# Decoder layer on one core: unread products in the opening waits, four contexts moved, an expert matrix folded into the second projection, and both gate halves in one operand

## What is computed

```
# 1. self-attention, B,T = 2,256 folded on (8,128) tokens; 32 heads of 16, 8 key/value heads, RoPE, causal
x = x + attn(layernorm(x), Wq, Wk, Wv, Wo)
# 2. cross-attention on ctx (8,128,512) joined with the layer-normalised x: 256 keys, 32 heads of 128, 4 key/value heads
x = x + xattn(layernorm(x), ctx, Wq, Wk, Wv, Wo)
# 3. feed-forward, on h = layernorm(x)
logits = h @ gate_w                                # 512 x 8
r      = sum(top_k(logits, 2))                     # one number a token
shared = relu(h @ up_w) ** 2 @ down_w              # 512 -> 1024 -> 512
routed = ((h @ fc1_w) @ expert_w) * r @ fc2_w      # 512 -> 256 -> 256 -> 512
x = x + layernorm(shared + routed) * gamma + beta
```

## Time and profile before

| | us |
|---|---|
| median of 3 runs (lowest, highest) | 1036.62 (1036.33, 1036.84) |
| the profiled execution, its own time | 1037.11 |
| its span, first to last instruction | 1035.4 |
| PE busy | 1015.5 (98% of the span) |
| DVE busy | 644.1 (62%) |
| ACT busy | 525.8 (51%) |
| POOL busy | 384.8 (37%) |
| mean granted TensorE clock | 0.998 |

### The profile page before, as it was taken

How to read it: one execution, slowest core, us unless ns; L and a number is a source line. 1 busy time by engine, 2 the same in 40 slices (tenths; PEclk the granted TensorE clock), 3 DMA queues, 4 the chain that set the end, 5 groups by cost and what they waited for, 6 DMA issues and landing times.

```text
span 1035.4 us, 15896 instructions
## 1 busy us (share of the span) xinstructions
PE 1015.5 (98%) x5656; PEld 854.4 (83%) x5656; DVE 644.1 (62%) x1305; ACT 525.8 (51%) x1593; POOL 384.8 (37%) x370
## 2 busy tenths in 40 slices
PE   6999999999999999999999999999999999999997
PEld 6777777777888888888888888888888888799996
DVE  6888888878435655556555456555546578466554
ACT  5666667666525645445455446454436556422211
POOL 3545444444132433224433225433226356311110
PEclk9999999999999999999999999999999999999999
DMA  9300111104552221202212102121202213100000
GB/s 336 113 21 22 41 41 42 41 21 143 164 154 68 65 71 42 91 22 68 65 41 72 62 26 87 42 82 32 71 32 82 91 62 103 42 1 20 20 21 21
DMA packets 70105, 68.38 MB, mean 66 GB/s; under 512 B 3984, under 2 KB 53904, under 8 KB 70032
## 3 DMA queue, kind: packets, MB, share of 16 engines
q1 hardware_dynamic: 70032, 67.43, 20.8%
HBM read 48.55 MB, written 18.87 MB: 65 GB/s over the span
## 4 chain that ended last, share of the span: by engine, by line
PE 94%; DVE 3%; DMA 1%; issue 1%; ACT 0%; SPq 0%; DVEq 0%; POOLq 0%; POOL 0%
PE bank L224 27%; PE bank L226 26%; PE bank L225 26%; PE bank L981 5%; PE bank L753 3%; PE bank L715 1%; PE bank L719 1%; DVE b_nb L1591 1%; DMA rawQ<-in_L_attn_Wq_dram 1%; PE bank L722 1%; PE bank L725 1%; PE bank L633 0%; DVE b_max L1588 0%; DVE PTl L1345 0%; PE bank L668 0%
## 5 line engine op out<-in xcount | busy, mean ns | idle before, releaser
L570 POOL TENSOR_TENSOR Pb<-Pb,b_rec 128x512 f32<-128x512 f32 x128 | 133.6, 1044 | 349.8 <-DVE b_rec L1595 348.6
L1588 DVE TENSOR_REDUCE b_max<-bank 128x2 f32<-128x512 f32 x128 | 87.8, 686 | 84.4 <-PE bank L226 84.2
L1087 ACT ACTIVATE PTh<-bank 128x512 fp32r<-128x512 f32 x128 | 76.2, 595 | 115.5 <-PE bank L981 114.8
L1229 ACT ACTIVATE Pb<-bank,b_nb 128x256 f32<-128x256 f32 x256 | 119.2, 475 | 15.7 <-DVE b_nb L1591 15.5
L1144 ACT ACTIVATE Pa<-bank,a_nb 128x128 f32<-128x128 f32 x256 | 90.4, 367 | 42.9 <-DVE a_nb L1468 42.1
L224 PE MATMUL bank<-WOh,Oh 128*128 128x512 f32 x256 | 110.7, 432 | 1.0 <-DVE x_res L1605 0.9
L532 POOL TENSOR_TENSOR Pa<-Pa,a_rec 128x512 f32<-128x512 f32 x64 | 68.2, 1066 | 104.6 <-DVE a_rec L1474 104.0
L224 PE MATMUL bank<-XTh,WQh 128*128 128x512 f32 x256 | 101.6, 397 | 0.0
L226 PE MATMUL bank<-WOh,Ol 128*128 128x512 f32 x256 | 100.9, 394 | 0.0
L225 PE MATMUL bank<-WOl,Oh 128*128 128x512 f32 x256 | 100.4, 392 | 0.0
L226 PE MATMUL bank<-XTh,WQl 128*128 128x512 f32 x256 | 100.0, 390 | 0.0
(11 more groups left out here) (230 smaller groups left out, 2706.3 us busy)
## 6 DMA issues: line engine op xcount, KB each, us to landing
kv_scratch<-KVst SPq DMA_DIRECT2D x64, 256.0 KB, 2.9
KV<-kv_scratch SPq DMA_DIRECT2D x32, 512.0 KB, 3.4
raw<-in_L_xattn_Wo_dram SPq DMA_DIRECT2D x32, 256.0 KB, 3.3
raw<-in_L_xattn_Wq_dram SPq DMA_DIRECT2D x24, 256.0 KB, 4.0
cx<-in_ctx_dram SPq DMA_DIRECT2D x8, 256.0 KB, 9.1
raw_first<-in_L_xattn_Wq_dram SPq DMA_DIRECT2D x8, 256.0 KB, 4.7
raw<-in_L_ffn_up_w_dram SPq DMA_DIRECT2D x8, 256.0 KB, 4.0
raw<-in_L_ffn_down_w_dram SPq DMA_DIRECT2D x8, 256.0 KB, 2.6
```

What stands on the lines that cost most here:

```text
L570: gp.tensor_tensor(pk, pk, b_rec[:, k % 4, :].unsqueeze(2).to_broadcast([P, 2, KEYS]), ALU.mult).then_inc(b_g_norm, 1)
L1087: return act.activation(dst, src, ACT.Copy)
L1229: op = act.activation(Pb[:, k % 4, h, :], bank[k % 3][:, h * KEYS:(h + 1) * KEYS], ACT.Exp, bias=b_nb[:, k % 4, h:h + 1], scale=X_SCALE, a ...
L1588: dve.tensor_reduce(b_max[:, k % 4, :], bank[k % 3][:].rearrange("p (h k) -> p h k", h=2), AX.X, ALU.max).then_inc(b_v_mx, 1)
```

## The change

Six edits are made together.

1. DVE makes `ident_r`, the identity in float32r, first of all, and fills its two zeroed value buffers after it. PE then begins with `warm_up(9, 7)`: nine products of 512 columns of the identity with itself into bank 7, which nobody reads, ahead of its wait for the first weights; and `warm_up(7, 1)`, seven such products into bank 1, behind `turn_xn(0)`, ahead of the wait for the query weights.
2. In the opening PE makes the second half of `unit(0)` ahead of `turn_k(0)` and not behind it, and the contexts 4, 5 and 6 ahead of `unit(3)`; ACT and DVE take these contexts' parts accordingly, ahead of the parts of unit 3.
3. The expert matrix is not split as it comes. It is loaded apart (`ex_raw`), transposed in four pieces at the end of step 26 of the last group (`turn_expert`), split, and multiplied with `fc2` once (`expert_product`, 12 products of 512 columns, ahead of `out_piece(g, 7, 0)`). The result, split again, takes the place of `fc2`. The expert product of every pair, its high part on ACT and its low part on DVE go away, and the last product takes `LTh`, `LTl` directly.
4. The gate's high and low part lie in one operand `GT`, in columns 0 to 7 and 8 to 15, so that two multiplications a chunk do for three; DVE adds the two halves of the logits with a reduction where it had copied them.
5. `LN3_STEPS` are 8 and 12 where they were 14 and 16.
6. The down weights of the last group take the steps 26 to 30 where they had 27 to 31, the expert weight step 26.

```diff
@@ PE, the opening
+            def warm_up(count, bk):
+                for _ in range(count):
+                    pe.matmul(bank[bk][:].rearrange("p (c k) -> p c k", c=SG), ident_r[:],
+                              ident_r[:].unsqueeze(1).to_broadcast([P, SG, P]), start=True, stop=True)
+
+            pe.wait_ge(v_c, 1)
+            warm_up(9, 7)
             pe.wait_ge(g_const, 6)
             pe.wait_ge(ld_kv, 32)
             for n in range(2):
                 turn_weights(n)
             turn_xn(0)
+            warm_up(7, 1)
             pe.wait_ge(ld_q, 16)
...
             turn_q(0)
+            unit(0, (2, 3))
             turn_k(0)
-            unit(0, (2, 3))
             unit(1)
...
             scores(0, 1)
-            unit(3)
             pe.wait_ge(v_w, 10)
             turn_context(4)
             turn_context(5)
             turn_context(6)
+            unit(3)
+
             pe.wait_ge(v_ul, 3)
             turn_context(7)
@@ PE, the last group and the feed-forward
+            def turn_expert():
+                pe.wait_ge(b_v_q, XG + 2 * XG * XKV - XG)
+                pe.wait_ge(ld_ex, 16)
+                for mc in range(LC):
+                    for lc in range(LC):
+                        op = pe.transpose(bank[6][:, mc * LAT + lc * P:mc * LAT + (lc + 1) * P],
+                                          ex_raw[:, lc, mc * P:(mc + 1) * P], ident[:])
+                op.then_inc(c_pe_e, 1)
+
+            def expert_product():
+                pe.wait_ge(c_v_e, 1)
+                pe.wait_ge(b_a_exp, DUOS * XKV)
+                pe.wait_ge(b_g_w, ffn_ready(NUP + NFC - 1))
+                for lc, bk in enumerate((6, 1)):
+                    for mc in range(LC):
+                        op = split3(pe, bank[bk][:], EXTh[:, mc, lc * P:(lc + 1) * P], EXTl[:, mc, lc * P:(lc + 1) * P],
+                                    F2h[:, mc, :], F2l[:, mc, :], mc == 0, mc == LC - 1)
+                op.then_inc(c_pe_e, 1)
...
+                    if last and k == EX_STEP:
+                        turn_expert()
+                if last:
+                    expert_product()
                 out_piece(g, NB - 1, 0)
                 outputs(g, QUADS - 1)
...
                 for kc in range(KC):
-                    op = split3(pe, bank[0][:, 0:KEYS], GTh[:, kc, :], GTl[:, kc, :], X3h[:, kc, :], X3l[:, kc, :],
-                                kc == 0, kc == KC - 1)
+                    pe.matmul(bank[0][:, 0:KEYS], GT[:, kc, :], X3h[:, kc, :], start=kc == 0, stop=False)
+                    op = pe.matmul(bank[0][:, 0:KEYS], GT[:, kc, :], X3l[:, kc, :], start=False, stop=kc == KC - 1)
...
-                    if n == 1:
-                        pe.wait_ge(b_g_w, ffn_ready(NUP + NFC))
-                        pe.wait_ge(c_v_l, 2 * c + 1)
-                        for m in range(LC):
-                            for kc in range(LC):
-                                op = split3(pe, bank[1][:, m * KEYS:(m + 1) * KEYS], EXh[:, kc, m * P:(m + 1) * P],
-                                            EXl[:, kc, m * P:(m + 1) * P], LTh[:, kc, :], LTl[:, kc, :],
-                                            kc == 0, kc == LC - 1)
-                        op.then_inc(c_pe_e, 1)
-                pe.wait_ge(c_v_l, 2 * c + 2)
+                pe.wait_ge(c_v_l, c + 1)
@@ DVE
+            dve.wait_ge(g_const, 5)
+            dve.tensor_copy(ident_r[:], ident[:]).then_inc(v_c, 1)
+            dve.wait_ge(g_const, 6)
+            dve.tensor_copy(mask_r[:], mask_f[:]).then_inc(v_c, 1)
             dve.memset(f32(Vbdh[:]), 0.0).then_inc(v_c, 1)
             dve.memset(f32(Vbdl[:]), 0.0).then_inc(v_c, 1)
-            dve.wait_ge(g_const, 6)
-            dve.tensor_copy(ident_r[:], ident[:]).then_inc(v_c, 1)
-            dve.tensor_copy(mask_r[:], mask_f[:]).then_inc(v_c, 1)
...
+                        if k == EX_STEP:
+                            dve.wait_ge(c_a_e, 1)
+                            lo(EXTl[:].rearrange("p m n -> p (m n)"), bank[6][:],
+                               EXTh[:].rearrange("p m n -> p (m n)")).then_inc(c_v_e, 1)
+                if last:
+                    for lc, bk in enumerate((6, 1)):
+                        dve.wait_ge(c_a_e, 2 + lc)
+                        lo(F2l[:, lc, :], bank[bk][:], F2h[:, lc, :]).then_inc(c_v_e, 1)
                 outputs(g, QUADS - 1)
...
-                        dve.tensor_copy(logits[:], bank[0][:, KEYS:2 * KEYS].rearrange(
-                            "p (t n) -> p t n", t=2)[:, :, 0:NE])
+                        halves = bank[0][:, KEYS:2 * KEYS].rearrange("p (t s n) -> p t n s", t=2, n=NE)[:, :, :, 0:2]
+                        dve.tensor_reduce(logits[:], halves, AX.X, ALU.add)
@@ SP, behind the self-attention
             sp.dma_start(gate_raw[:], gate_w.rearrange("(k p) n -> p k n", p=P)).then_inc(ld_gate, 16)
+            sp.dma_start(ex_raw[:], expert_w.rearrange("(k p) n -> p k n", p=P)).then_inc(ld_ex, 16)
```

More of the change, by code:

```diff
@@ L193, in decoder_layer @@
         HBl = sb("HBl", "Q", 24, [IC, KEYS], F32R)
-        EXh = sb("EXh", "KV", 8, [LC, LAT], F32R)
-        EXl = sb("EXl", "KV", 10, [LC, LAT], F32R)
+        EXTh = sb("EXTh", "KV", 8, [LC, LAT], F32R)
+        EXTl = sb("EXTl", "KV", 10, [LC, LAT], F32R)
         xn3 = sb("xn3", "F", 0, [2, D])
-        GTh = sb("GTh", "F", 4, [KC, P], F32R)
-        GTl = sb("GTl", "F", 6, [KC, P], F32R)
+        GT = sb("GT", "F", 4, [KC, P], F32R)
+        ex_raw = sb("ex_raw", "F", 6, [LC, LAT])
         gate_raw = sb("gate_raw", "F", 8.5, [KC, NE])
@@ L297, in chunk_steps @@
                 steps += [(22 + i - NUP, "ffn", i) for i in range(NUP, NUP + NFC)]
-                steps += [(26, "ffn", NUP + NFC)]
-                steps += [((17, 19, 21, 27, 28, 29, 30, 31)[c], "ffn", NUP + NFC + 1 + c) for c in range(IC)]
+                steps += [((17, 19, 21, 26, 27, 28, 29, 30)[c], "ffn", NUP + NFC + c) for c in range(IC)]
             return sorted(steps, key=lambda step: step[0])
@@ L335, in query_cell @@
             return t[:, b % HALF, h, i, :] if b // HALF else t[:, i, h, b % HALF, :]
-        LN3_STEPS = (14, 16)
+        LN3_STEPS = (8, 12)
+        EX_STEP = 26
         U_START = [("k", 0, g, 0, 6 + g % 2) for g in range(XKV)]
@@ L1007, in _ @@
             pe.wait_ge(b_g_w, ffn_ready(NUP + NFC - 1))
-            pe.wait_ge(c_v_g0, 3)
+            pe.wait_ge(c_v_g0, 2)
+            pe.wait_ge(c_v_e, 3)
             def pair(c, last):
@@ L1201, in _ @@
             k_hi(0)
-            act.wait_ge(v_c, 2)
+            act.wait_ge(v_c, 4)
             values_hi(0)
@@ L1213, in _ @@
             probs(0, 1)
+            for b in range(4, NB - 1):
+                context_hi(b)
+            probs(0, 2)
             unit_hi(3)
-            probs(0, 2)
-            for b in range(4, NB):
-                context_hi(b)
+            context_hi(NB - 1)
             for b in range(NB):
@@ L1255, in _ @@
             act.wait_ge(ld_gate, 16)
-            act.wait_ge(c_v_g0, 2)
-            hi(GTh[:, :, 0:NE], gate_raw[:]).then_inc(c_a_g, 1)
+            act.wait_ge(c_v_g0, 1)
+            hi(GT[:, :, 0:NE], gate_raw[:]).then_inc(c_a_g, 1)
             def outputs(g, q):
@@ L1304, in group @@
                     split_weights(k)
+                    if last and k == EX_STEP:
+                        act.wait_ge(b_pe_pv, QUADS * g + 12)
+                        act.wait_ge(c_pe_e, 1)
+                        hi(EXTh[:].rearrange("p m n -> p (m n)"), bank[6][:]).then_inc(c_a_e, 1)
+                if last:
+                    act.wait_ge(c_pe_e, 2)
+                    for lc, bk in enumerate((6, 1)):
+                        hi(F2h[:, lc, :], bank[bk][:]).then_inc(c_a_e, 1)
                 outputs(g, QUADS - 1)
-                split_weights(DUOS)
             for g in range(XKV):
@@ L1576, in _ @@
             maxima(0, 2)
-            unit_lo(3)
+            for b in range(4, NB - 1):
+                context_lo(b)
             dve.wait_ge(ld_x, 16)
             ln1_stats(1)
-            for b in range(4, NB):
-                context_lo(b)
+            unit_lo(3)
+            context_lo(NB - 1)
             ln1(1)
@@ L1605, in residual @@
                 dve.tensor_tensor(x_res[:, b, :], x_res[:, b, :], bank[7][:], ALU.add).then_inc(b_v_x, 1)
-            dve.memset(f32(GTh[:]), 0.0).then_inc(c_v_g0, 1)
-            dve.memset(f32(GTl[:]), 0.0).then_inc(c_v_g0, 1)
-            dve.wait_ge(c_v_g0, 2)
+            dve.memset(f32(GT[:]), 0.0).then_inc(c_v_g0, 1)
+            dve.wait_ge(c_v_g0, 1)
             dve.sem_inc(b_v_pt, 2)
```

19 lines of the change are left out of this document (4 added, 15 removed).

## The result

| | before | after |
|---|---|---|
| median, us (lowest, highest; runs) | 1036.56 (1036.33, 1036.84; 4) | 1030.91 (1030.25, 1031.03; 4) |
| profiled execution, own time | 1037.11 | 1030.99 |
| its span | 1035.4 | 1029.3 |

The ratio is 0.9944, 95% interval 0.9927 to 0.9961: 5.65 us faster. 1031.0 was forecast.

A forecast was written before the change was run, and what follows sets the result against it. PE was taken as the bound, holding 94% of the last-ending chain. Opening -3.2, last group +1.9 and feed-forward -4.3 sum to -5.6 us, taking the median from 1036.6 to 1031.0; range 1029.3 to 1033.0.

The forecast's parts named there:

- The opening: Fills and new order in the opening: fast query transposes, fewer waits; -3.2 us, bounds -1.5 to -4.2.
- POOL's step ahead of the fourth turn: POOL's normalisation at 49.34 comes 2.7 us earlier, cutting PE's lead from 3.9 to 3.2 us.
- rival B: Opening: DVE is the bound from the keys on, gain stays below -2 us; about 1032.6; 13%.
- The step that failed: Opening: PE's higher clock level comes 4.4 us after PE starts, so at 6.4 us with fills from 2.0.
- rival A: Opening: clock level changes late or not for transposes, fills overrun to 11.9, only about -1.5 left; 1032.7; 13%.
- The last group: Four transposes and 12 products added on PE, partly filling the residual's wait; +1.9 us, between +1.4 and +2.7.
- the two open terms: Last group: DVE's late maximum of step 29, 0 to +0.4 us; statistics moved to 8 and 12, -0.4 to 0.
- The feed-forward: Gate and expert products removed; three pairs give 0.8 each after new xn waits, the last 1.91; -4.3 us.
- rival C: Feed-forward: PE's new wait for xn does not appear, gain is 7.6 us; 1027.7; 6%.
- D: Feed-forward: waits of about 1 us in three pairs drop PE to its lower clock level; 1037.6; 3%.
- E: Whole change: parts don't do what they say, within 0.2% nothing is left; 4%.

The follow-up runs named there:

- kernel 1: Kernel before plus only DVE's identity first and the nine and seven unread fill products; 1037.29 us, ratio 0.9993.
- kernel 3: Kernel before plus only the gate's high and low part in one operand; 1035.86 us, ratio 0.9986.
- kernel 4: Changed kernel with the fills and the new opening order undone; 1034.29 us, ratio 0.9968 to the kernel before.
- kernel 2: Kernel before plus only the new opening order (second half of unit 0 before the keys' transposes, contexts 4 to 6 before unit 3); 1035.08 us, ratio 0.9973.
- kernel 10: Changed kernel without fills, ident_r made behind the memsets as before; 1031.47 us, ratio 0.9946 to the kernel before.
- kernel 6: Changed kernel without the second fill of seven products; 1030.81 us, ratio 0.9934 to the kernel before.
- kernel 7: Changed kernel with the one-time expert product behind out_piece(g, 7, 0), not ahead; 1032.46 us, ratio 0.9950 to the kernel before.
- kernel 9: The changed kernel run once more, unaltered; 1031.23 us, ratio 0.9945 to the kernel before.
- kernel 11: Changed kernel with next pair's statistics one block earlier and one fill of 16 products for 9 and 7; 1029.33 us, ratio 0.9927 to the kernel before.
- kernel 12: Changed kernel with LN3_STEPS back at 14 and 16; 1031.41 us, ratio 0.9945 to the kernel before.
- kernel 5: Changed kernel with fills made of identity transposes (19 and 16) in place of products; 1031.45 us, ratio 0.9935 to the kernel before.
- kernel 8: Changed kernel with the next pair's statistics and normalisation one block earlier on DVE; 1028.65 us, ratio 0.9914 to the kernel before.

## Why the prediction was right, and where it wasn't

**The opening: -3.2 forecast, -3.12 in the profile.** The total, and how it is bound, came out: POOL's `XKl` at 16.13 (16.2 forecast), set by the landing of `rawXK` at 15.4; `xn` of batch 1 ending at 41.36 (41.3); the fourth turn at 47.75 (47.7); first product at 2.14 (2.0); query transposes (11.84 - 10.04) / 16 = 0.11 apart. POOL's step ahead of the fourth turn, at which the lead was to be cut, begins at 46.66 for 49.34, 2.68 earlier (2.7 forecast), and ends at 47.70, just ahead of the turn. The way from `XKl`'s start to the fourth turn is fixed by the order, within 0.3:

| | `XKl` starts | fourth turn | between |
|---|---|---|---|
| before; 1; 3; 4 | 17.23; 17.72; 16.79; 17.28 | 50.87; 51.41; 50.48; 50.94 | 33.64 to 33.69 |
| after; 2; 10 | 16.13; 16.76; 16.57 | 47.75; 48.42; 48.23 | 31.62 to 31.66 |
| 6; 7; 9; 11; 12 | 17.00; 16.12; 16.12; 16.24; 16.59 | 48.63; 47.76; 47.74; 47.89; 48.23 | 31.62 to 31.65 |
| 5; 8 | 17.49; 16.01 | 48.88; 47.42 | 31.39; 31.41 |

So the order gives 2.0 to 2.3 in every profile, and the earlier start of `XKl` gives the other 1.1 of this pair of profiles. That part is luck in some measure: with the changed order the fourth turn lies anywhere from 47.42 to 48.88, 2.0 to 3.5 ahead of the earlier trace rows, and -3.2 was met because the profile of the changed kernel is among the early ones. DVE's smaller lead (rival B) did not hold it back.

**The step that failed is the one that gives the clock's part to the fills.** "Before, it changed level 4.4 us after it set in at 10.01; the same from 2.0 is 6.4" reads a law from one event, as the prediction itself says under rival A. From the distances, the level came at about 14.4 in the first profile and in kernel 4, at 12.6 in kernel 3, at 10.8 in kernel 2 and before 10.34 in kernel 10, all without fills and with nearly the same work. With fills it came at about 5 in kernels 1 and 12, at about 5.5 in kernel 11, at about 7 in the changed kernel (6.7) and in 7 and 9, by 7.2 in kernel 8, and only at about 11 in kernels 5 and 6. There PE began on the weights late (7.49 and 7.84); but so it did in 1, 8 and 12 (7.89, 7.18, 7.28), so that alone doesn't explain it.

The Trainium skill (TensorE: Matmul & The Clock Gate, Part 1: The HAM clock gate) has it that how many of a kernel's first products are slow varies from run to run of the same kernel. The traces agree: the kernels before, 3 and 4 have the same opening, and their level came 1.8 us apart. The prediction didn't weigh that rule.

What the early level can give is bounded besides: once the transposes are fast enough for ACT to be free when `rawXK` lands, nothing more comes. Kernels 2 and 10 reach that without fills: the `XKl` of kernel 10 at 16.57 waits for the transfer too. In nine of the fourteen profiles ACT stands waiting for `rawXK`, and there its landing alone, from 15.30 (kernel 8) to 16.29 (kernel 6), sets `XKl`'s start; the landing varies by nearly as much as the fills gave in the first pair of profiles. Fills are thus worth up to 1.1 us by the run, nothing in others, and in kernel 1 they cost; between the medians of kernels 9 and 10 it is 0.24, which is inside the scatter. Even the 0.49 by which kernel 9 leads at the fourth turn is gone at the first gate product, 899.41 in both. How often the kernel before has a late level stays open, since only one of its runs has a trace; and it was not tried to set the level apart from the landing of the weights.

**The last group: +1.9 forecast, +1.49 measured from the fourth turn on.** The forecast's own terms don't give +1.9 in the middle: 0.43 + 1.9 is 2.3, and the two open terms (0 to +0.4 and -0.4 to 0) cancel; +1.9 takes the best of one and nothing of the other, and the lower bound of +1.4 has no term at all. So part of the miss was already made up by that choice. The product is 891.48 - 888.75 = 2.73 (2.75 forecast), and no wait for the residual is left. Two terms were mis-sized: what the residual's wait was worth, and the waits for `PTl`. A row's idle time begins at the modelled end of the row before, while the products ahead of it stood 0.23 apart, so a wait costs more than it shows. A step of the last group takes 845.27 - 841.35 = 3.92 in kernel 10 without a wait. In the changed kernel it takes 4.38, and only 0.20 of that is shown as idle (PE's timeline after):

```profile
840.92 0.60 PE L1013 MATMUL bank<-ident,Pb 128*128 128x128 f32 x4
...
843.80 0.50 PE L223 MATMUL bank<-PTh,KV 128*128 128x512 f32 x1 [0.20 <-DVE PTl L1378]
...
845.30 0.60 PE L1013 MATMUL bank<-ident,Pb 128*128 128x128 f32 x4
```

So each wait costs its row and 0.26. The residual's 0.87 was worth 1.13, not 0.87; kernel 7 shows it (+1.23). And the last group has three waits for `PTl` of 0.2 now, where it had four, one of them 0.41: 1.38 for 2.05 us. With 0.4 for the transposes: 2.73 + 0.4 - 1.13 - 0.67 = 1.3 to 1.4, and the 0.1 that remains was lost ahead of the last group (the lead of 3.01 at 840.92). About 0.2 of the 0.67 is edit 5 (kernel 12). The waits themselves come and go, why was not found out: kernels 1 and 3 have three of them with the old steps where the kernel before has four, so part of the 1.49 is chance; kernel 10 has two, and so makes good at the gate (899.41) what it was behind at the fourth turn.

**The feed-forward: -4.3 forecast, -4.49 measured.** The new wait for the second `xn` is there in the three pairs, 0.83 to 0.84 in the rows and 950.88 - 949.03 = 1.85 for eight transposes that took 0.79: 1.06. The chain from the first `hr` to the second `xn` went from 12.84 to 949.87 + 0.55 - 937.62 = 12.80, so it neither shrank nor grew by the reduction. Pairs are 31.25, 31.17 and 31.18 long for 32.12, 32.02 and 32.02, 0.84 to 0.87 less (0.8 forecast), the last gives 1.93 (1.91). This is where the remaining gain of rival C lies, and kernel 8 got about three fifths of it.

**The rivals.** A's size did not come, but its mechanism appeared in kernel 1, and in kernels 5 and 6 the level came late. B and C are refuted by the fourth turn and the pairs (B only for this profile: in kernel 5 the opening's gain was 1.99). D did not happen: behind the 0.84 us of idling in pair 1 the 48 products take 961.88 - 950.88 = 11.00 us, 0.229 each, the higher level. A longer pause was followed by a fall in kernel 1 (2.11 us). E has nothing for it.

**The sum.** -3.12 + 1.49 - 4.49 = -6.12 in the profiles for -5.6 forecast; the medians moved by 5.65, since the first profile lay 0.5 above its median and this one 0.1. The forecast was close for the median partly by that luck, and by the opening's.

## What to carry to other kernels

Before warming an engine's clock with idle products, look at which transfer bounds the stretch and at more than one trace of the start: in this kernel the level came by itself in time in two of five traces without fills (2 and 10), and the fills could not bring more than the transfer allowed. When a reordered or removed product shortens PE's path next to a chain over three engines, count both: here 1.06 of the 1.91 us removed from a pair turned into a wait, and starting the chain earlier, not shortening it, won three fifths of that back, until the next step in DVE's queue was late.

## What the runs showed of the hardware

- The first weights, the last of them issued at 1.72 or 1.73 us in every kernel, let PE begin on them anywhere from 5.46 us (kernel 10) to 7.89 (kernel 1).
- Float32 transposes alone were enough for the higher level: in kernel 5 they went from 0.216 us apart to 0.109 with nothing else run before.
- A pause of 2.11 us behind fast products was followed by a granted clock of 0.50, which set in only after PE had worked again for about 0.5 us. Pauses of 0.83 us (kernel 8) and 1.43 us (kernel 12) behind fills had fast products behind them, pauses of 1.37 us (kernel 5) and 1.49 us (kernel 6) slow ones. In 5 and 6 the fills had been slow to the end (4.31 and 4.21 us), but in 8 too (4.21), so what tells them apart is not shown.
- The column of the granted clock says 1.00 for 2.14 to 6.14 us, where products of 512 columns lie 0.444 apart, in the changed kernel and in kernel 6, and of the openings shows 0.50 only for the fall in kernel 1. In these traces only the distances tell the level at the start.
- A wait of PE that a row shows as 0.20 cost 0.46 from start to start, one shown as 0.87 about 1.1.
